# Two layer norms of a linear-attention and mixture-of-experts kernel: the reciprocal square root moved from ScalarE to VectorE

## What is computed

```python
q = elu(x @ Wq.T + bq) + 1;  k = elu(x @ Wk.T + bk) + 1;  v = x @ Wv.T + bv
for each chunk of 128 tokens, per head:      # causal linear attention, state S and z
    num = tril(q @ k.T) @ v + q @ S
    den = sum(q * (cumsum(k) + z))
    out = num / den
    S, z = S + k.T @ v, z + sum(k)
x1 = layernorm(x + out @ Wo.T + bo)           # (x - mean) / sqrt(var + 1e-5)
g  = softmax(x1 @ gate_w.T + gate_b);  w = g where g is among the top 2, else 0
y  = layernorm(x1 + sum over experts e of w[e] * (x1 @ expert_w[e].T + expert_b[e]))
```

## Time and profile before

| what | value |
|---|---|
| two timed runs | 2897.32 and 2971.55 us, median 2934.43 |
| the profiled execution, slowest core | 2894.26 us |
| its span, first to last instruction | 2892.7 us (cores: 2880.7 to 2892.7) |
| PE busy | 1916.3 us (66%) |
| DVE busy | 983.6 us (34%), 1456 instructions |
| ACT busy | 524.8 us (18%), 668 instructions |
| granted PE clock, mean | 0.781 to 0.786 of full speed |

### The profile page before, as it was taken

The page is one execution under the profiler, slowest core; times in us unless marked ns, Lnnn a source line. Parts: engine busy times, 40 slices in busy tenths (PEclk is TensorE's granted clock), DMA queues, the critical chain, the costliest instruction groups (busy, mean ns, idle before and its releaser), DMA issues.

```text
span 2892.7 us, 26493 instructions; the slowest of 8 cores (2880.7 to 2892.7 us)
## 1 busy us (share of the span) xinstructions
PE 1916.3 (66%) x10144; PEld 929.7 (32%) x10144; DVE 983.6 (34%) x1456; ACT 524.8 (18%) x668; POOL 143.3 (5%) x264
## 2 busy tenths in 40 slices
PE   2355554664697548874597657974498746976496
PEld 0122222232343323333243323433243332433243
DVE  0233322333233333433234333334234332343333
ACT  1321111132003210132103210032101320032100
POOL 1000000100000000100000000000001000000000
PEclk8676787876798659976698768986699857987698
DMA  5620366420343103520144103521135202441031
GB/s 179 237 103 15 138 232 232 146 80 8 111 140 128 59 37 133 171 82 15 66 152 160 51 8 126 152 102 58 58 124 167 81 8 87 143 148 52 31 110 71
DMA packets 63346, 303.93 MB, mean 105 GB/s; under 512 B 8172, under 2 KB 8428, under 8 KB 43766
## 3 DMA queue, kind: packets, MB, share of 16 engines
q1 hardware_dynamic: 34326, 163.80, 17.2%
q0 software_dynamic: 28896, 138.43, 13.1%
HBM read 260.26 MB, written 41.94 MB: 104 GB/s over the span
## 4 chain that ended last, share of the span: by engine, by line
PE 55%; DVE 12%; ACT 12%; DMA 11%; issue 8%; DVEq 0%; POOL 0%; ACTq 0%; SPq 0%; POOLq 0%
PE q L850 28%; PE q L694 6%; PE q L374 6%; DMA wb<-ewT 4%; PE q L446 4%; DMA xtl<-xT 3%; ACT etmp L390 2%; PE q L700 2%; PE q L452 2%; PE q L513 2%; PE q L751 2%; ACT L779 1%; ACT L728 1%; ACT etmp L395 1%; ACT wb L259 1%
## 5 line engine op out<-in xcount | busy, mean ns | idle before, releaser
L850 PE MATMUL q<-wb,x1t_bf 128*128 128x512 bf16 x4096 | 927.6, 391 | 132.7 <-DVE x1f L864 64.8
L850 PEld LDWEIGHTS q<-wb,x1t_bf 128*128 128x128 bf16 x4096 | 408.6, 100 | 654.5 <-issue 199.2
L864 DVE SCALAR_TENSOR_TENSOR x1f<-q,w_all,x1f 128x1024 f32<-128x1024 f32 x256 | 328.2, 1283 | 545.9 <-PE q L850 545.9
L374 PE MATMUL q<-xt_bf,wb 128*128 128x512 bf16 x1024 | 244.0, 403 | 166.8 <-ACT etmp L395 114.9
L694 PE MATMUL q<-wb,attnTb 128*128 128x512 bf16 x512 | 167.6, 500 | 79.6 <-ACT attnTb L685 79.6
L374 PEld LDWEIGHTS q<-xt_bf,wb 128*128 128x128 bf16 x1024 | 103.8, 102 | 306.5 <-issue 201.2
L909 ACT ACT_TABLE_LOAD x8 | 10.3, 1283 | 937.9 <-DVE mnv L907 937.9
L194 POOL DMA_DIRECT2D wb<-escr x126 | 67.6, 537 | 1763.9 <-PE q L850 791.4
L513 PE MATMUL q<-qt_bf,ktz 128*128 128x128 bf16 x512 | 53.3, 286 | 146.9 <-DVE qtz L491 146.9
L533 DVE TENSOR_TENSOR msc_bf<-q,maskT_f 128x1024 bf16<-128x1024 f32 x64 | 75.4, 1220 | 187.0 <-PE q L513 187.0
L714 DVE TENSOR_TENSOR x1f<-q,x0c 128x1024 f32<-128x1024 f32 x32 | 39.2, 1224 | 281.9 <-PE q L700 281.9
(11 more groups left out here) (83 smaller groups left out, 1661.5 us busy)
## 6 DMA issues: line engine op xcount, KB each, us to landing
wb<-escr SPq DMA_DIRECT2D x70, 1024.0 KB, 6.7
wb<-escr POOLq DMA_DIRECT2D x70, 1024.0 KB, 8.9
wb<-ewT SPq DMA_DIRECT2D x16, 2048.0 KB
escr<-wb SPq DMA_DIRECT2D x12, 2048.0 KB, 7.8
xtl<-xT POOLq DMA_DIRECT2D x64, 256.0 KB, 3.2
x0c<-x POOLq DMA_DIRECT2D x32, 512.0 KB, 4.9
out<-osb POOLq DMA_DIRECT2D x32, 512.0 KB, 4.1
wb<-escr SPq DMA_DIRECT2D x56, 256.0 KB, 3.1
```

The costliest lines, as they stand in the source:

```text
L374: fn = lambda e, src=src, k=k, f=f: e.matmul(quad[f // 2][:, (f % 2) * 512:(f % 2 + 1) * 512], src[:, k * 1024 + f * 128: k * 1024 + (f + ...
L850: fn = lambda e, src=src, k=k, c=c, qi=qi, hh=hh: e.matmul(quad[qi][:, hh * 512:(hh + 1) * 512], x1t_bf[:, c * 1024 + k * 128: c * 1024 + ...
L864: e.scalar_tensor_tensor(x1f[:, c * 1024:(c + 1) * 1024], quad[qi][:], w_all[:, c * 8 + e_i: c * 8 + e_i + 1], x1f[:, c * 1024:(c + 1) * 1 ...
```

## The change

A helper `rsqrt_dve` computes 1/sqrt(var + eps) on DVE alone. It starts from an integer estimate (a constant, 0x5F3759DF, less the bits of the argument shifted right by one) and refines it by two Newton steps. It has 13 DVE instructions on one element in each of the 128 partitions; each waits for the one before it. It takes the place of ACT's square root and DVE's reciprocal in both layer norms. All else stays as it is; POOL gets one more memset at the start.

```diff
+    magic_c = sb("magic_c", [128, 1], mybir.dt.int32)
+    rsq = [sb(f"rsq{j}", [128, 6], F32) for j in range(3)]
...
+    B.op("POOL", lambda e: e.memset(magic_c[:], 0x5F3759DF), inc="cpl")
...
+    def rsqrt_dve(var_ap, out_ap, scr, wait_ev):
+        B.waits("DVE", wait_ev)
...
+        v = B.op("DVE", lambda e: e.tensor_scalar(
+            ve, var_ap, eps_c[:, 0:1], None, ALU.add), inc="cdv")
+        B.wait("DVE", "cdv", v)
+        v = B.op("DVE", lambda e: e.tensor_scalar(
+            vh, ve, 0.5, None, ALU.mult), inc="cdv")
+        B.wait("DVE", "cdv", v)
+        v = B.op("DVE", lambda e: e.tensor_scalar(
+            yb.bitcast(mybir.dt.int32), ve.bitcast(mybir.dt.int32), 1, None,
+            ALU.arith_shift_right), inc="cdv")
+        B.wait("DVE", "cdv", v)
+        v = B.op("DVE", lambda e: e.tensor_tensor(
+            yy.bitcast(mybir.dt.int32), magic_c[:, 0:1],
+            yb.bitcast(mybir.dt.int32), ALU.subtract), inc="cdv")
+        for _ in range(2):
+            B.wait("DVE", "cdv", v)
+            v = B.op("DVE", lambda e: e.tensor_tensor(ya, yy, yy, ALU.mult),
+                     inc="cdv")
+            B.wait("DVE", "cdv", v)
+            v = B.op("DVE", lambda e: e.tensor_tensor(yb, ya, vh, ALU.mult),
+                     inc="cdv")
+            B.wait("DVE", "cdv", v)
+            v = B.op("DVE", lambda e: e.tensor_scalar(
+                yc, yb, 1.5, -1.0, ALU.subtract, op1=ALU.mult), inc="cdv")
+            B.wait("DVE", "cdv", v)
+            v = B.op("DVE", lambda e: e.tensor_tensor(yy, yy, yc, ALU.mult),
+                     inc="cdv")
+        B.wait("DVE", "cdv", v)
+        v = B.op("DVE", lambda e: e.tensor_copy(out_ap, yy), inc="cdv")
+        return v
...
-        B.wait("ACT", "cdv", vagg)
-        vsq = B.op("ACT", lambda e, j=j: e.activation(
-            sdev[j][:], mnv[j][:, 1:2], AF.Sqrt, bias=eps_c[:, 0:1]), inc="cac")
-        B.wait("DVE", "cac", vsq)
-        vrs = B.op("DVE", lambda e, j=j: e.reciprocal(rstd[j][:], sdev[j][:]),
-                   inc="cdv")
-        B.wait("DVE", "cdv", vrs)
+        vrsq = rsqrt_dve(mnv[j][:, 1:2], rstd[j][:], rsq[j], [("cdv", vagg)])
+        B.wait("DVE", "cdv", vrsq)
...
-            B.wait("ACT", "cdv", vagg)
-            vsq = B.op("ACT", lambda e: e.activation(
-                sdev2[:], mnv2[:, 1:2], AF.Sqrt, bias=eps_c[:, 0:1]), inc="cac")
-            B.wait("DVE", "cac", vsq)
-            vrs = B.op("DVE", lambda e: e.reciprocal(rstd2[:], sdev2[:]),
-                       inc="cdv")
-            B.wait("DVE", "cdv", vrs)
+            vrsq2 = rsqrt_dve(mnv2[:, 1:2], rstd2[:], rsq[2], [("cdv", vagg)])
+            B.wait("DVE", "cdv", vrsq2)
```

More of the change, by code:

```diff
@@ L469, in proj_core @@
         free_and_feed(2)
+    def rsqrt_dve(var_ap, out_ap, scr, wait_ev):
+        B.waits("DVE", wait_ev)
+        ve = scr[:, 0:1]
+        vh = scr[:, 1:2]
+        ya = scr[:, 2:3]
+        yb = scr[:, 3:4]
+        yc = scr[:, 4:5]
+        yy = scr[:, 5:6]
+        v = B.op("DVE", lambda e: e.tensor_scalar(
[27 more added lines that the diff above has]
+        return v
     def build_zmask(c):
```

## The result

The changed kernel is slower: 2967.14 us, median of 11 runs, against 2899.92 us for the kernel before, median of 10 runs. The ratio is 1.0216, with a 95% interval of 1.0184 to 1.0249: +63 us, from 53 to 72. So it is slower beyond the scatter, but whether by more than 2% is not settled. (The ratios, and the medians given for experiments, leave out runs in which one half of the chip ran at a lower clock than the other.) The profiled execution took 2977.3 us.

A forecast was written before the change was run, and what follows sets the result against it. It took PE alone to bound the experts' stage, and a chain hopping between engines, including ACT's table loads, the chunks' stage. 52.8 - 41.1 + 46.6 + 2 + 10.4 = +70.7 us on 2894.3 gave 2965, range 2915 to 3012.

The forecast's parts named there:

- One root: Each new reciprocal root on DVE: 2.20 us busy plus 14 gaps of 0.106, 3.69 us; 3.76 in the second layer norm.
- The upper bound: Most one root might cost: inner gaps of 0.18 add 0.96 us, 0.231 for four immediate TENSOR_SCALARs adds 0.26, 4.9 us.
- C: Rival: small instructions cost more, inner gaps of 0.18 us on 61 roots, +59, 3024 us (3040 with 0.231 immediates); chance 0.12.
- First norm and gate: Chunks' stage, 32 times each: first layer norm +1.65 us, +52.8 in all; gate's table load gone, 1.283 each, -41.1.
- Borders: Six superblock borders after the first: second norm outruns 1.5 us of cover, +8.8 each, 52.6, less 6.0 buffer waits, +46.6.
- First border: First superblock border: third Exp +1.3 us if the output DMA lands when it did, +3.0 if 1.65 later; +2 taken.
- End: After the last expert nothing covers the four second layer norms: +10.4 us.
- ACT's load at L390 lies beside PE: At the borders, ACT's own table load at L390 vanishes, but it lay beside PE, so no gain was counted.
- PE's clock: Longer waits fall where PE already runs at half clock: cost nil; a lighter gate letting it rise sooner not excluded.
- Rival A: Not slower: the root's 12 inner gaps vanish as DVE overlaps instructions, root 2.42 us, sum -7, 2887 us; chance 0.08.
- Rival B: Second norm stays hidden beside the q projection, so the borders' 48.6 us vanish, 2916 us; chance 0.08.

## Why the prediction was right

It gave 2965 us and 2.4% slower; the runs say 2967 and 2.2%. That the times agree within 2 us is in part luck: the sum of the changes was 6 us too large (+70.7; the traces show 65), and it started from an execution 6 us below the median of the kernel before (2894.3 and 2899.9). The mechanism and the terms held. By its own steps:

- **One root.** 3.69 us predicted (3.76 in the second norm), 3.57 (3.64) measured in 49 of the 64 roots; 14 take 0.13 to 0.36 us more, and one waits for a buffer. The gap of 0.106 taken from the gate's chain was right; the instructions are 154 to 160 ns, not 165. The pointer's 60 ns came out as 60 (214 against 154 for the same instruction with an immediate). The upper bound was read less well: 0.231 for TENSOR_SCALARs with immediates is the duration of one with a pointer, and the 0.96 us for wider gaps count 13 inner gaps where there are 12 (0.89). Both make only C too dear, its 3024 by 5 us and its 3040 by 20.
- **First norm and gate.** +52.8 predicted; 32 x (3.57 - 2.04) = 49.0 by the typical case. The gate's -41.1 is right: its wait fell by 60.4 - 19.5 = 40.9 us. The net of 12 was measured as +16 with the first norm changed alone, and the stretches of the two traces show +9. PE's idle time before L513 rose from 7.63 to 9.17 us, where 9.3 was predicted.
- **Borders.** +8.8 each predicted, 8.5 measured. Of buffer waits 6.0 us were to be given back, and 5.4 were: the three borders that had waits grew by 20.1 instead of 25.5. The second norm alone gave +60 us.
- **First border.** +2 predicted, +0.2 measured on the slowest cores; over the eight cores the mean is 38.5 us before and 39.8 after, +1.2. The choice between "lands when it did" and "lands 1.65 later as issued" was the first of the two, because POOL issued chunk 0's output late in both kernels. It had loads of weights before it in its list. Here are the application and the issue, before and after:

```profile
529.09 0.81 DVE L916 TENSOR_SCALAR osb<-x1f,mnv,rstd 128x1024 f32<-128x1024 f32 x1
543.58 1.07 POOL L194 DMA_DIRECT2D out<-osb  x2
...
548.68 0.81 DVE L947 TENSOR_SCALAR osb<-x1f,mnv,rstd 128x1024 f32<-128x1024 f32 x1
561.21 1.07 POOL L196 DMA_DIRECT2D out<-osb  x2
```

  The issue comes 17.9 and 17.5 us after PE's start on q, 13.7 and 11.7 after the application's end, so a later application did not move it. DVE's wait fell from 17.0 to 8.7 us.
- **End.** +10.4 predicted, +10.2 measured from the end of the last expert to the start of the last application (13.1 and 23.2 us).
- **ACT's load at L390 lies beside PE.** This step was wrong for the kernel before: it held up the first Exp by 1.28 us at each border, as the kernel without table switches showed. It did no harm to the sum, since in the changed kernel the third Exp waits for DVE (9.62 us at the border shown) and the gain is lost in that wait.
- **PE's clock.** Nil predicted; the mean of the changed kernel's cores is 0.781 to 0.786, as before, and the first 3 us of k's projection run at 0.50 at every border of both. In the chunks' stage, though, it did differ, which the prediction had named as a sign against itself: from a superblock's first residual addition to its fourth the granted clock is 0.61 to 0.63 before and 0.64 after (means of each core over seven superblocks). So "nil" was not quite right there. It had left open that the lighter gate lets the clock rise sooner. The stretch grew from 95.6 to 96.3 us even so, and what the higher clock gave back was not separated.

Rival A (no gaps) named a real mechanism with the wrong condition. DVE does overlap small instructions, even more than A assumed, but only when nothing waits for them. Rival B (the second norm stays hidden) is out by 163.1 against 113.7 us of waits, rival C by starts 0.26 us apart.

## What to carry to other kernels

Ask of each place where an instruction stands what covers it there, not what it costs on the average: the same root cost 0.25 us net in the first norm (+1.53, less a load of 1.28 at the gate) and 2 to 3 us in the second, because the second had 1.5 us of cover left and a table load to win back in only one root of four. A chain of small DVE instructions cost some 0.26 us for each result that is waited for, against 0.76 to 0.86 us for the way over ACT without a table load. As an estimate from the durations and gaps measured here, two such instructions take 0.7 us and can win, and three take 0.95 and can't. Where the complaint is a table switch, first look for functions of one table that give the same value, and then for the next wait behind it, which here was the output buffer.

## What the runs showed of the hardware

- Independent DVE instructions on one element a partition start 0.07 us apart while each lasts 0.154; dependent ones with a semaphore wait start 0.26 apart. I had expected 0.16 or less for the first.
- Ln and Exp share a table with Relu and Copy in this build: one ACT_TABLE_LOAD in the whole kernel.
- An activation on one element a partition takes 0.29 us with a pointer as its bias (Sqrt, Ln and Relu) and 0.20 without one (Exp); the second starts 0.09 us after the first has ended, though it waits for it.
- In 14 of the 64 roots of the changed kernel the way from bn_aggr to the application is 0.13 to 0.36 us longer than in the others, without a wait for anything that the profile names. They are the same 14 roots, held at the same instruction by the same time within 0.01 us, on core 2 and in the second trace of the kernel. So it goes with the place in the program and is not chance. What holds DVE there was not tried.
